# A graph's second layer: turn of ELU at a step's beginning, attention added between bend and mask, fills one step earlier

## What is computed

```python
def gat_layer(x, adj, W, a_self, a_neigh, b):
    feat = jnp.einsum('nf,hfo->hno', x, W)
    e = leaky_relu(attn_self[:, :, None] + attn_neigh[:, None, :], 0.2)
    e = e + MASK_VAL * (1.0 - adj)[None, :, :]
    alpha = jax.nn.softmax(e, axis=-1)
    out = jnp.einsum('hnm,hmo->hno', alpha, feat) + b[:, None, :]
    return jax.nn.elu(concat_heads(out))

x = x + tanh(g_xattn[0]) * gat(gat(ctx_512, layernorm(x)), layernorm(x))
xt = layernorm(x)
x = x + tanh(g_ffn[0]) * (sum over 2 of 8 experts of weight * expert(xt) + sum of 2 shared experts(xt))
```

## Time and profile before

| | |
|---|---|
| median of 3 runs | 406.56 us (405.89 to 406.83) |
| the profiled execution | 405.61 us, of which the span is 403.8 us |
| PE busy | 364.5 us (90%) |
| DVE busy | 251.8 us (62%) |
| ACT busy | 217.9 us (54%) |
| POOL busy | 83.2 us (21%) |
| chain that ended last | PE 79%, DVE 12%, ACT 4% |
| stream, step 16 to the last weigh | 82.8 to 171.3 us |
| routed tiles | from 241.7 us on |

### The profile page before, as it was taken

The page is one execution under the profiler, slowest core; times in us unless marked ns, Lnnn a source line. Parts: engine busy times, 40 slices in busy tenths (PEclk is TensorE's granted clock), DMA queues, the critical chain, the costliest instruction groups (busy, mean ns, idle before and its releaser), DMA issues.

```text
span 403.8 us, 8136 instructions
## 1 busy us (share of the span) xinstructions
PE 364.5 (90%) x2668; PEld 319.1 (79%) x2669; DVE 251.8 (62%) x831; ACT 217.9 (54%) x512; POOL 83.2 (21%) x93
## 2 busy tenths in 40 slices
PE   6985874775999899999999999999999999999991
PEld 5663553554888788788888889999999999999980
DVE  1896999999877987882665424445444444444430
ACT  3879999896858648421111246454545555454310
POOL 7705140001000010107142000222213131313131
PEclk9999899899999999999999999999999999999997
DMA  6149498625004000099888221323232323332121
GB/s 183 47 183 391 210 296 316 265 83 211 0 32 183 0 2 28 0 354 419 339 335 291 37 43 36 39 41 41 41 41 40 39 40 40 45 43 27 23 25 14
DMA packets 30499, 48.69 MB, mean 121 GB/s; under 512 B 18640, under 2 KB 27008, under 8 KB 27520
## 3 DMA queue, kind: packets, MB, share of 16 engines
q1 hardware_dynamic: 25152, 41.92, 29.9%
q0 software_dynamic: 4080, 5.18, 8.1%
q10 hardware_dynamic: 1232, 1.15, 0.9%
HBM read 39.46 MB, written 8.77 MB: 119 GB/s over the span
## 4 chain that ended last, share of the span: by engine, by line
PE 79%; DVE 12%; ACT 4%; issue 2%; DMA 1%; POOL 0%; DVEq 0%; POOLq 0%
PE ps_c L797 20%; PE ps_o L815 12%; PE ps_c L662 12%; PE ps_pt L669 6%; PE ps_n L797 5%; PE ps_pt L579 5%; DVE weights L1086 5%; PE ps_n L662 4%; DVE weights L1102 3%; PE ps_o L594 3%; PE ps_f L568 2%; PE ps_n L669 2%; ACT weights L895 2%; ACT weights L901 1%; PE ps_n L536 1%
## 5 line engine op out<-in xcount | busy, mean ns | idle before, releaser
L797 PE MATMUL ps_c<-tile_t,weights 128*128 128x128 f32 x736 | 89.5, 275 | 0.0
L797 PEld LDWEIGHTS ps_c<-tile_t,weights 128*128 128x128 f32 x736 | 87.5, 192 | 1.2
L1152 DVE SCALAR_TENSOR_TENSOR gate_silu<-gate_tanh,ps_c 128x256 f32<-128x256 f32 x76 | 31.9, 420 | 81.9 <-ACT gate_tanh L999 66.9
L492 POOL DMA_INDIRECT out<-y_sb,tile_in x23 | 35.7, 1554 | 146.7 <-DVE y_sb L1340 146.7
L895 ACT ACTIVATE weights<-weights 128x256 f32<-128x256 f32 x128 | 63.1, 498 | 1.1 <-DVE weights L1102 1.0
L662 PE MATMUL ps_c<-x_norm_t,weights 128*128 128x256 f32 x240 | 56.6, 383 | 1.3 <-DVE hidden L1155 1.3
L1004 ACT ACTIVATE weights<-weights 128x2560 f32 x23 | 53.6, 2337 | 7.4 <-issue 7.4
L1086 DVE SCALAR_TENSOR_TENSOR weights<-weights 128x256 f32<-128x256 f32 x128 | 53.5, 480 | 5.6 <-ACT weights L882 4.5
L579 PE MATMUL ps_pt<-ident,weights 128*128 128x128 f32 x256 | 37.2, 293 | 20.2 <-ACT weights L901 20.2
L815 PE MATMUL ps_o<-weights,hidden 128*128 x230 | 53.6, 380 | 0.6 <-DVE hidden L1155 0.6
L579 PEld LDWEIGHTS ps_pt<-ident,weights 128*128 128x128 f32 x256 | 31.5, 152 | 26.3 <-issue 25.5
(11 more groups left out here) (183 smaller groups left out, 456.8 us busy)
## 6 DMA issues: line engine op xcount, KB each, us to landing
weights<-w_routed SPq DMA_DIRECT2D x8, 1920.0 KB, 14.4
weights<-t_rows SPq DMA_DIRECT2D x14, 1024.0 KB, 5.6
weights<-w_shared SPq DMA_DIRECT2D x1, 3840.0 KB, 15.5
tile_in<-slots SPq DMA_DIRECT2D x92, 32.0 KB, 1.8
slots<-pad_row SPq DMA_DIRECT2D x1, 1188.0 KB, 11.4
slots<-pad_row SPq DMA_DIRECT2D x8, 132.0 KB, 2.9
weights<-x SPq DMA_DIRECT2D x2, 256.0 KB, 3.1
x_in<-x SPq DMA_DIRECT2D x2, 256.0 KB, 4.3
```

Source lines behind the costliest of these rows:

```text
L492: pool.indirect_dma_start(out=out, out_offset=bass.IndirectOffsetOnAxis(ap=tile_in[:, slot, ID_COL:ID_COL + 1].bitcast(U32), axis=0), in_= ...
L797: mm = pe.matmul(ps_chunk[c][:, part * cw + i * P:part * cw + (i + 1) * P], ring[r % RING][:, a:a + P], tile_t[:, r % 2, k, :], start=(k = ...
```

## The change

On TensorE `turn_h1` goes from the end of the step with u = 1 to its beginning, right behind turn(w). On VectorE `add_attention` goes from behind mask_max to between bend (and the first slot's piece) and mask_max of the same step. Turning and copying the normalised rows, the router and the two choices go one step ahead, and so do both fills: 18 and 26, 19 and 27, 28 and 29, and FIRST_FILL 19, SECOND_FILL 27. `FILLED` becomes 9, so one piece of graph 1 is left behind the stream, and the order there is written anew. `end_elu` and `normalise` stay in their places.

```diff
-TURN_X_NORM = {step_after(n, UNITS - 1): n for n in range(PAIR)}
-COPY_X_NORM = {step_after(n, UNITS): n for n in range(PAIR)}
-CHOOSE = {step_after(PAIR - 1, UNITS + 1 + k): k for k in range(TOPK)}
+TURN_X_NORM = {step_after(n, UNITS - 2): n for n in range(PAIR)}
+COPY_X_NORM = {step_after(n, UNITS - 1): n for n in range(PAIR)}
+CHOOSE = {step_after(PAIR - 1, UNITS + k): k for k in range(TOPK)}
...
-FIRST_FILL = step_after(0, UNITS)
-SECOND_FILL = step_after(1, UNITS)
+FIRST_FILL = step_after(0, UNITS - 1)
+SECOND_FILL = step_after(1, UNITS - 1)
...
                 turn(w)
+                if u == 1 and second_layer(L - 1):
+                    if routers_before(w) > 0:
+                        pe.wait_ge(router_exped, routers_before(w))
+                    turn_h1(L - 1)
                 if slots_now and slots_now[0]:
                     filler(slots_now[0])
...
                     spread_inverse(L)
-                if u == 1 and second_layer(L - 1):
-                    if routers_before(w) > 0:
-                        pe.wait_ge(router_exped, routers_before(w))
-                    turn_h1(L - 1)
                 if w in TURN_X_NORM:
...
             turn_x_norm(2)
-            shared_piece(1, FILLED)
+            for i in range(FILLED, PIECES):
+                shared_piece(1, i)
             pe.wait_ge(invb_copied, STREAM)
             ranks(0, ps_f)
-            shared_piece(1, FILLED + 1)
+            shared_down(1, 0, 0)
             pe.wait_ge(x_norm_copied, 3)
             turn_h1(LAST)
-            shared_piece(1, FILLED + 2)
+            shared_down(1, 0, 1)
             pe.wait_ge(ranks_read, 1)
             router(2, ps_f)
-            for e, half in itertools.product(range(NSH), range(HV)):
-                shared_down(1, e, half)
+            shared_down(1, 1, 0)
+            shared_down(1, 1, 1)
...
             copy_x_norm(2)
-            shared_tanh(1, FILLED)
+            for i in range(FILLED, PIECES):
+                shared_tanh(1, i)
             elu_exponent(LAST)
-            for i in range(FILLED + 1, PIECES):
-                shared_tanh(1, i)
-                if i == FILLED + 2:
-                    router_exponent(2, ps_f)
+            router_exponent(2, ps_f)
...
                 if slots_now:
                     filled_piece(slots_now[0])
+                if u == 1 and second_layer(L - 1):
+                    add_attention(ORDER[L - 1][0])
                 if u == 2 and second_layer(L - 1):
                     normalise(ORDER[L - 1][0])
...
                     end_elu(L - 1)
-                if u == 1 and second_layer(L - 1):
-                    add_attention(ORDER[L - 1][0])
...
             divide(LAST)
-            tail_piece(1, FILLED)
+            for i in range(FILLED, PIECES):
+                tail_piece(1, i)
             end_elu(LAST)
             place(0, ps_f)
-            tail_piece(1, FILLED + 1)
             add_attention(3)
-            tail_piece(1, FILLED + 2)
             normalise(3)
```

## The result

The changed kernel takes 418.57 us (median of 4 runs, 418.45 to 418.80); the ratio to the kernel before is 1.0272 (95% interval 1.0233 to 1.0311). The kernel before had a fourth run beside it, of 413.77 us, which moves its median from 406.56 to 406.69. The profiled execution took 418.51 us, span 416.7. The forecast was 414.7 with a range to 417.2: slower was right, its size was not, and the time lies 1.4 us outside the range.

A forecast was written before the change was run, and what follows sets the result against it. TensorE was taken to bound the kernel, its waits costing full length from step 20. -1.9 + 1.5 + 1.7 + 3.5 = +4.8 us, plus 3.3 for two clock falls, gives +8.1 on 406.56: 414.7 us, range 410.8 to 417.2.

The forecast's parts named there:

- What bounds the kernel, and that the waits cost their length: From step 20 on TensorE has fill in every step, so a wait in its queue costs its full length.
- The wait in step 17 and its size: TensorE's turn_h1 in step 17 waits 2.8 us for end_elu, costing only what reaches step 20.
- The walk from there to turn(21): Adding durations on TensorE from step 17: turn(21) ends at 108.8, against 110.7 before with piece (0,2) included.
- the gain of 1.9: Moving the fills one step ahead saves 1.9 us by turn(21), 1.65 of half clock before included.
- Steps 21, 25 and 29: TensorE's waits: +1.5 us for a piece in step 21, +1.7 and +3.5 for end_elu in 25 and 29.
- the sum at full clock: All terms without falls of the clock: -1.9 + 1.5 + 1.7 + 3.5 = +4.8 us.
- The clock: Half clock behind two of TensorE's three gaps (2.8, 3.0, 3.5 us): +3.3 us; chance of two falls 0.39.
- The base: The sum was added to 406.56 us, the median of the kernel before; its profiled execution took 405.61.
- That the turn would not wait: Rival: end_elu is done before TensorE reaches the turn, the three waits go, -0.4 or -1.9 us (404.7); chance 0.05.
- the waits would be absorbed: Rival: VectorE or ScalarE bounds the stream after step 20, TensorE's waits are made up, no change; chance 0.04.
- Three falls: Rival: the clock falls behind all three gaps on TensorE, +9.8 us in all, 416.4 us; chance 0.25.

The follow-up runs named there:

- e5: Changed kernel, TensorE's idle time up to step 18 and inside its three waits for end_elu filled with turns of the identity: 410.29 us, ratio 1.0074.
- e6: Kernel before, TensorE's idle time up to step 18 and ahead of the spread in step 19 filled with turns of the identity: 404.33 us, ratio 0.9906.
- e2: Kernel before with one edit, TensorE's turn of ELU right behind turn(w): 415.96 us, ratio 1.0219.
- e4: Changed kernel with TensorE's idle time up to step 15 filled with turns of the identity that nobody reads: 416.79 us, ratio 1.0226.
- e3: Kernel before with TensorE's idle time up to step 15 filled with turns of the identity that nobody reads: 406.46 us, ratio 0.9980.
- e1: Changed kernel with the turn of ELU and the attention back in their old places, the fills still one step ahead: 410.27 us, ratio 1.0071.
- e8: Changed kernel; on VectorE in steps with u = 0 the first slot's piece goes ahead of divide and end_elu ahead of mask_max: 408.91 us, ratio 1.0029.
- e10: Kernel before with VectorE's order as in e8 and turns of the identity in TensorE's idle time: 401.90 us, ratio 0.9840.

## Why the prediction was right and wrong

**What bounds the kernel, and that the waits cost their length.** Right. e5 against e6 shows it with the clock taken out from step 16 on.

**The wait in step 17 and its size.** Right, 2.91 for 2.8. *The walk from there to turn(21)* is right within half a microsecond at full clock: turn(17) to turn(21) is 22.25 in e5, and in e6 18.86 + 3.56 for the two pieces = 22.42, so the stretch ahead is worth 0.2. I had written that the gain of 1.9 contains 1.65 us of half clock of the kernel before, and did not draw the conclusion that the change's own share is 0.3. In the profiled pair the term came out at +1.1, where -1.9 and one fall of 1.65 were forecast: with the changed kernel at full clock it would have been -1.3 (22.25 against 23.56), and 6.8 us of half clock cost 2.4 (24.68 against 22.25).

**Steps 21, 25 and 29.** Right, within 0.25 us each. These three are 6.3 us of the 12.9. With 0.2 to 0.3 for steps 17 to 21 in place of 1.9 the sum at full clock is 6.1 to 6.4, and e5 and e6 lie 6.0 apart.

**The clock.** The term was mis-sized, and its mechanism was right in steps 25 and 29 only. I counted two falls of 3.3 us, a loss of 3.3; in the profiled run the two from step 17 on cost 2.4 and 1.7, 4.1 together. The fall in step 29 followed its wait. The one in step 17 began within the wait and lasted 6.8 us (10.2 in e2, 10 in e4), and falls in step 17 came without any wait for end_elu too (3.4 us in e3, 6.8 in e1). The early turn stood beside the longest of them, but what starts them is not shown, and neither is what sets their length. That the number of falls came out as forecast was luck. Of the Trainium skill's rule ("TensorE: Matmul & The Clock Gate", section "Why this matters for your kernels": idle gaps between bursts bring back half clock) the runs bear out the wait in step 29, and that in step 25 in part: behind its 2.93 us the clock held in the profiled run, and it fell behind the same wait in e4 and behind one of 3.4 in e2.

**The stretch before step 16.** This is the step that failed outright: the sum has no term for it, since its code is the same. It brought 3.2 us up to turn(16) and 3.5 up to turn(17), at 23.8 us of half clock for 6.8. e3 and e4 show that the clock made it: with TensorE kept busy turn(16) comes at 82.45 and 82.19. TensorE is idle there again and again (in the kernel before eight times for ScalarE's copy alone, 14.7 us in all between 35 and 82 us). That a small shift decides whether the next microseconds run at half clock is argued, not shown. The two profiles run within 0.13 us of each other until step 5, where the same eight transposes took 1.07 before and 1.94 after. Of the kernel before,

```profile
39.24 1.07 PE L579 MATMUL ps_pt<-ident,weights 128*128 128x128 f32 x8 [1.71 <-ACT weights L901]
```

and of the kernel after

```profile
39.18 1.94 PE L579 MATMUL ps_pt<-ident,weights 128*128 128x128 f32 x8 [1.69 <-ACT weights L902]
```

**The base.** The three runs shown of the kernel before (405.89 to 406.83) were from its fast end. In the runs beside the experiments its medians were 408.21, 407.81, 407.65 and 408.33, with single runs from 405.56 to 414.33, and the mean granted clock goes roughly with the time: 0.98 at 406, 0.96 to 0.97 at 408, 0.96 at 411, 0.946 at 414.33. Against 407.8 the changed kernel is 10.8 slower, which is 6.0 at full clock and 4.8 more loss by half clock than the kernel before has (8.3 against 3.5; the 418.57 was not measured beside the others, so a few tenths are uncertain). So a part of the 12.9 us between the two profiles is the choice of the profiled run: with 405.61 us and a mean granted clock of 0.982 it was at the fast end too, 2.2 below 407.8. And with 407.8 as its base the same sum would have forecast 415.9, still 2.7 short. What stays open is what sets, in a given kernel, where the first fall of the clock comes; the changed kernel came out within 0.35 us in all four runs, the one before did not.

**The rivals.** That the turn would not wait, and that the waits would be absorbed, are both out. "Three falls", 416.4, was the nearest of the cases, but only by its number: the profiled run had two falls from step 17 on, and what was missing was the stretch before step 16.

## What to carry to other kernels

Before a wait is moved ahead in an engine's queue, count on the releasing engine what stands between the common event and the release: here 6.1 us of VectorE against 2.7 to 3.1 of TensorE. The move was made on the side that waits, while the lever was the order on the side that releases (e8, e10). And in a stretch where TensorE is often idle, the clock can move the time by microseconds between kernels whose code there is the same (3.2 us here); a pair of runs with the idle time filled tells what a change costs by itself. A fall near a wait is not yet a fall by that wait: look whether the kernel without the wait has it too, as e3 has.

## What the hardware showed that I had not expected

- Filling TensorE's idle time with products that nobody reads makes the kernel faster, 407.81 to 404.33 us, where TensorE had only been waiting; no instruction of use was removed or moved.
- The same code ran 3.2 us apart up to step 16, with 6.8 and 23.8 us of half clock, and the mean granted clock of the kernel before goes from 0.946 to 0.982 over its runs with a time from 414.33 to 405.56.
- Falls lasted 3.4, 6.8, 10 and 13.4 us. The longer ones are not only those in which TensorE went on waiting for others: in the 7.0 us from 57.8 on of the kernel after, and in the 6.7 from 88.2 on of e1, its rows show it busy throughout, at half clock.
